# Nine one-hot tables and single-sample grams in a DLRM interaction tower

## The reference

```python
e = stack([tbl_t[ids[:, t]] for t in range(26)], axis=1)         # 2048 x 26 x 128
combined = concatenate([dense[:, None, :], e], axis=1)           # 2048 x 27 x 128
inter = einsum('bfd,bgd->bfg', combined, combined)[:, iu, ju]    # 351 pairs, iu < ju
h = concatenate([dense, inter, dense], axis=1)                   # 607 columns
h = maximum(h @ W_top1 + b_top1, 0)                              # 512
h = maximum(h @ W_top2 + b_top2, 0)                              # 256
y = h @ W_top3                                                   # 1
```

## Time and profile before

| | us |
|---|---|
| median of three runs | 413.59 (409.7 to 418.95) |
| profiled execution | 417.99 |
| its span in the trace | 416.2 |
| PE busy | 375.6 |
| DVE busy | 259.6 |
| POOL busy | 277.9 |
| ACT busy | 117.8 |

### The profile page before, as it was taken

The page is one execution under the profiler, slowest core; times in us unless marked ns, Lnnn a source line. Parts: engine busy times, 40 slices in busy tenths (PEclk is TensorE's granted clock), DMA queues, the critical chain, the costliest instruction groups (busy, mean ns, idle before and its releaser), DMA issues.

```text
span 416.2 us, 7055 instructions
## 1 busy us (share of the span) xinstructions
PE 375.6 (90%) x2906; PEld 339.9 (82%) x2906; DVE 259.6 (62%) x377; ACT 117.8 (28%) x255; POOL 277.9 (67%) x295
## 2 busy tenths in 40 slices
PE   0779998697989999999999999999999998889897
PEld 0768998697979898789879896989889886776787
DVE  4799989477766767577757585767657240521420
ACT  2442234222242232222332221322332132231120
POOL 6787778777777777777777777777777777720000
PEclk9999999999999999999999999999999998999856
DMA  7999444444333345334343444335333342310000
GB/s 178 262 280 257 106 98 91 77 78 92 78 78 60 73 91 101 83 81 90 78 82 77 89 83 102 79 56 116 56 53 52 56 78 51 58 25 2 1 2 0
DMA packets 51294, 35.91 MB, mean 86 GB/s; under 512 B 6488, under 2 KB 45016, under 8 KB 51264
## 3 DMA queue, kind: packets, MB, share of 16 engines
q0 software_dynamic: 41472, 18.89, 25.8%
q1 hardware_dynamic: 9792, 16.58, 15.4%
HBM read 35.44 MB, written 0.01 MB: 85 GB/s over the span
## 4 chain that ended last, share of the span: by engine, by line
POOL 42%; PE 38%; issue 15%; DMA 3%; ACT 1%; DVE 1%; POOLq 0%
POOL E L264 42%; PE psG L382 10%; PE psB L355 7%; PE psB L435 5%; PE psB L442 5%; PE psB L395 4%; DMA E<-tbl,gidx 2%; PE psB L340 2%; PE psB L428 2%; PE psB L449 1%; PE psB L411 1%; DVE Zp_lo L649 0%; ACT ET L541 0%; DMA gidx<-gather_idx 0%; ACT Zp_hi L571 0%
## 5 line engine op out<-in xcount | busy, mean ns | idle before, releaser
L264 POOL DMA_INDIRECT E<-tbl,gidx x288 | 277.2, 962 | 89.2 <-issue 86.5
L616 DVE TENSOR_TENSOR one_hot<-oidx,psR 125x1024 fp32r<-125x1024 int32 x128 | 152.5, 1216 | 44.0 <-PE psB L355 39.8
L355 PE MATMUL psB<-one_hot,tab_hi 125*128 125x256 f32 x512 | 137.3, 302 | 16.4 <-DVE tab_lo L621 11.1
L355 PE MATMUL psB<-one_hot,tab_lo 125*128 125x256 f32 x512 | 129.7, 287 | 0.0
L355 PEld LDWEIGHTS psB<-one_hot,tab_hi 125*128 125x128 f32 x512 | 99.7, 195 | 18.5 <-issue 12.0
L382 PE MATMUL psG<-ET 128*108 128x108 f32 x1024 | 111.5, 264 | 1.0 <-issue 0.8
L382 PEld LDWEIGHTS psG<-ET 128*108 128x108 f32 x1024 | 106.5, 180 | 2.2 <-ACT Y L506 0.9
L638 DVE COPY_PREDICATED S<-own,psG 108x216 f32<-108x216 int32 x192 | 77.0, 401 | 42.5 <-ACT S L565 36.6
L355 PEld LDWEIGHTS psB<-one_hot,tab_lo 125*128 125x128 f32 x512 | 100.0, 195 | 0.2
L541 ACT COPY ET<-psB 128x512 f32<-128x512 f32 (+1 forms) x80 | 42.6, 544 | 61.1 <-PE psB L340 61.0
L565 ACT COPY S<-psG 108x216 f32<-108x216 f32 x64 | 21.7, 340 | 100.2 <-PE psG L382 99.8
(11 more groups left out here) (35 smaller groups left out, 165.6 us busy)
## 6 DMA issues: line engine op xcount, KB each, us to landing
oidx<-hot_idx SPq DMA_DIRECT2D x32, 256.0 KB, 3.5
E<-tbl,gidx POOLq DMA_INDIRECT x288
ET<-tbl SPq DMA_DIRECT2D x8, 448.0 KB
dense<-dense_pairs SPq DMA_DIRECT2D x8, 128.0 KB, 4.0
Zd<-dense_rows SPq DMA_DIRECT2D x4, 256.0 KB, 2.8
UH<-W_pairs SPq DMA_DIRECT2D x1, 768.0 KB, 11.8
S<-W_dense SPq DMA_DIRECT2D x1, 512.0 KB, 8.5
w<-W SPq DMA_DIRECT2D x1, 512.0 KB, 10.3
```

The source lines that it names most:

```text
L264: nc.gpsimd.indirect_dma_start(E[:, n % SLOTS, i, :], None, gathered[feature_and_tile(n, i)[0]].bitcast(f32r), bass.IndirectOffsetOnAxis(a ...
L355: product = nc.tensor.matmul(bank[:, t % 2 * DUO:(t % 2 + 1) * DUO], tab[0:ROWS_P, t, r, :], one_hot[0:ROWS_P, m % RING, kc, :], start=(r ...
L616: nc.vector.tensor_tensor(one_hot[0:ROWS_P, m % RING], ids, rows, ALU.is_equal).then_inc(hot_full[m % RING], 1)
```

## The change

- **Tables.** One table with 1250 rows (125 partitions x 10 rows) becomes a one-hot table too: nine of them, 17 gathered. 272 gathers instead of 288. A duo has 74 row groups instead of 64, in 19 chunks of three or four, so 1184 products of 256 columns instead of 1024. The ring of one-hot tiles has four places and DVE builds four ahead.
- **Grams.** Each sample has its own matmul: 26 columns loaded, 26 columns passed, read from `ET` with a step of four elements (16 bytes) since the four samples lie interleaved. The four of a j write to partitions 0, 32, 64 and 96 up. A fill is 16 j. ACT alone copies a fill, all samples in one instruction; the predicated copies are gone. The columns without a sample between 26 and 32 are cleared once by DVE.
- **Buffers.** `ET` is a ring of three tiles (32 j) instead of two duos; psB has five banks instead of three, psG two instead of four.
- **Rows.** The gathered rows and the identity that turns them are plain fp32, no longer fp32r.
- **Order.** Stage h takes the turns of tile h by a running number. The chunks of a later duo d run in stages 2d-1 and 2d: stage 0 has the 19 chunks of duo 0, stages 1 to 14 have 9 or 10 each. In stage 16 the last three parts of the large piece are mixed with the last grams and with the layers of the small piece.
- **Loads.** All nine raw tables are loaded at once into places of their own (the third tile of `ET`, `UH`, `S`, `w2`); SP waits for all of them to be split before it loads the weights.

```diff
-ROWS = 1000
-HOT_TABLES = 8
+HOT_TABLES = ((1000, 8), (1250, 1))
+ROWS_P = 125
...
-    M = GROUP * F
+    M = F - 1
+    LANE = P // GROUP
+    MT = P - LANE + M
...
-    G_SIZE = 8
+    G_SIZE = 16
...
-    RING = 3
+    ET_RING = 3
+    RING = 4
...
-    BANKS = 3
+    BANKS = 5
...
-            return grams + layers_of(h)
-        split = T_GROUPS // 2 + 1
-        turns = [("T", d * T_GROUPS + i) for i in (range(split, T_GROUPS) if late else range(split))]
-
-        hots = [("hot", d + 1, late * CHUNKS // 2 + c) for c in range(CHUNKS // 2)] if d + 1 < DUOS else []
+            first, second = layers(SUPERS - 1, 0)[-3:], layers_of(h)
+            return (grams[:1] + first[:1] + grams[1:] + first[1:2] + second[:2] + first[2:] + second[2:])
+        turns = turns_of(h)
+
+        hots = [("hot", d + late, c) for c in range(CHUNKS)] if d + late < DUOS else []
         if h == 0:
-            hots = [("hot", 0, c) for c in range(CHUNKS)] + hots
             return hots[:5] + spread(turns, hots[5:])
+        hots = hots[:CHUNKS // 2] if late else hots[CHUNKS // 2:]
...
-        E = sb("E", [P, SLOTS, 4, D], f32r)
-        ET = sb("ET", [P, 2, DUO // GROUP, F, GROUP], f32)
+        E = sb("E", [P, SLOTS, 4, D], f32)
+        ET = sb("ET", [P, ET_RING, TILE_J, F, GROUP], f32)
...
             def load_weights():
+                sp.wait_ge(lo_ready, NS)
...
-                    turned = nc.tensor.transpose(bank[:, i * P:(i + 1) * P].bitcast(f32r),
-                                                 E[:, n % SLOTS, i, :], ident_r[:, :])
+                    turned = nc.tensor.transpose(bank[:, i * P:(i + 1) * P],
+                                                 E[:, n % SLOTS, i, :], ident[:, :])
...
                 for a in range(G_SIZE):
-                    j = i * G_SIZE + a
-                    four = ET[:, d % 2, j].rearrange("p f s -> p (f s)")
-                    gram = nc.tensor.matmul(psG[g % 2][0:M, a // 4, a % 4 * M:(a % 4 + 1) * M],
-                                            four, four, start=True, stop=True)
+                    j = i % TILE_FILLS * G_SIZE + a
+                    for q in range(GROUP):
+                        gram = nc.tensor.matmul(psG[g % 2][q * LANE:q * LANE + M, a * M:(a + 1) * M],
+                                                ET[:, tile % ET_RING, j, 0:M, q],
+                                                ET[:, tile % ET_RING, j, 1:F, q], start=True, stop=True)
...
-                    turned = nc.tensor.transpose(bank[0:n, i * M:(i + 1) * M], S[0:M, js, c],
-                                                 ident[0:M, 0:M])
+                    turned = nc.tensor.transpose(bank[0:n, i * P:i * P + MT], S[0:MT, js, c - 1],
+                                                 ident[0:MT, 0:MT])
...
-            def empty_gram_first(d, i):
+            def empty_gram(d, i):
                 g = gram_number(d, i)
                 act.wait_ge(G_full[g % 2], g // 2 + 1)
-                nc.scalar.copy(gram_rows(d, i), gram_samples(g, 0)).then_inc(G_first[g % 2], 1)
+                nc.scalar.copy(gram_rows(d, i),
+                               psG[g % 2][0:MT, 0:G_SIZE * M].rearrange("p (a f) -> p a f", a=G_SIZE)
+                               ).then_inc(G_out[g % 2], 1)
...
-            def empty_gram(d, i):
-                g = gram_number(d, i)
-                dve.wait_ge(G_first[g % 2], g // 2 + 1)
-                for q in range(1, GROUP):
-                    mine = own[0:M, q:q + 1].bitcast(i32).unsqueeze(2).unsqueeze(3).to_broadcast([M, 2, 4, F])
-                    copied = nc.vector.copy_predicated(gram_rows(d, i), mine, gram_samples(g, q))
```

More of the change, by code:

```diff
@@ L28, in dlrm_program @@
     PARTS = M1 + M2 + 1
-    T_GROUPS = NG // 2
+    TILES = 2 * DUOS
+    T_GROUPS = TILES * NG // 4
     SLOTS = 5
-    G_SIZE = 8
+    G_SIZE = 16
     G_FILLS = DUO // GROUP // G_SIZE
[L34 to L38, removed]
-    RING = 3
-    ID_RING = 3
     TILE_J = P // GROUP
     TILE_FILLS = TILE_J // G_SIZE
+    ET_RING = 3
+    RING = 4
+    ID_RING = 3
     SPREAD_P = ROWS_P // 16 * 16
-    RAW = 6
-    BANKS = 3
+    BANKS = 5
+    TABLE_K = [table.shape[0] // ROWS_P for table in small]
+    TABLE_BASE = [sum(TABLE_K[:t]) for t in range(NS)]
+    K_KINDS = sorted(set(TABLE_K))
+    ROW_BASE = {k: sum(x for x in K_KINDS if x < k) for k in K_KINDS}
+    CHUNK_K = 4
+    CHUNK_LIST = []
+    for t, k in enumerate(TABLE_K):
+        pieces = -(-k // CHUNK_K)
+        ends = [k * (i + 1) // pieces for i in range(pieces)]
+        CHUNK_LIST += [(t, start, end - start) for start, end in zip([0] + ends, ends)]
+    CHUNKS = len(CHUNK_LIST)
+    HOT_FILLS = -(-NS // 2)
+    FILL_FIRST = [min(c for c in range(CHUNKS) if CHUNK_LIST[c][0] // 2 == i) for i in range(HOT_FILLS)]
+    FILL_LAST = [max(c for c in range(CHUNKS) if CHUNK_LIST[c][0] // 2 == i) for i in range(HOT_FILLS)]
+    FIRST = -(-2 * NG // 4) * 4
     COLUMNS = [range(1 + 4 * b, min(5 + 4 * b, F)) for b in range(-(-(F - 1) // 4))]
@@ L93, in layers_of, with turns_of @@
             own = layers(u, 0)[first[quarter]:first[quarter + 1]]
-            return own + (layers(SUPERS - 1, 0) if quarter == 3 else [])
+            return own + (layers(SUPERS - 1, 0)[:-3] if quarter == 3 else [])
         return layers(u, 0)[LAYERS_FROM[quarter]:LAYERS_FROM[quarter + 1]]
+    def turns_of(h):
+        return [("T", n) for n in range(T_GROUPS) if 4 * n // NG == h]
     def steps_of(h):
@@ L125, in place_fills @@
         for i, step in enumerate(STEPS):
-            if step[0] == "gram" or (step[0] == "hot" and step[2] % FILL_CHUNKS):
+            if step[0] == "gram" or (step[0] == "hot" and step[2] not in FILL_FIRST):
                 continue
@@ L257, in _ @@
             pool.wait_ge(gidx_in[0], 16)
-            for n in range(DUOS * T_GROUPS):
-                if n == T_GROUPS:
+            for n in range(T_GROUPS):
+                if n == FIRST // 4:
                     pool.wait_ge(gidx_in[1], 16)
@@ L278, in load_table @@
             def load_table(h):
-                rows = small[h].rearrange("(p k) d -> p (k d)", k=ROWS_K)
+                rows = small[h].rearrange("(p k) d -> p (k d)", k=TABLE_K[h])
                 for part in (slice(0, SPREAD_P), slice(SPREAD_P, ROWS_P)):
                     sp.dma_start(raw_table(h)[part], rows[part]).then_inc(table_in[h], 16)
-            first = T_GROUPS * 4
-            sp.dma_start(gidx[:, 0:first], gather_idx[:, 0:first]).then_inc(gidx_in[0], 16)
+            sp.dma_start(gidx[:, 0:FIRST], gather_idx[:, 0:FIRST]).then_inc(gidx_in[0], 16)
             load_oidx(0)
-            for h in range(RAW):
+            for h in range(NS):
                 load_table(h)
@@ L308, in _ @@
                 for step in steps_of(h):
-                    if step[0] == "hot" and step[2] % FILL_CHUNKS == FILL_CHUNKS - 1:
-                        n = chunk_number(step[1], step[2]) // FILL_CHUNKS + ID_RING
-                        if n < DUOS * CHUNKS // FILL_CHUNKS:
+                    if step[0] == "hot" and step[2] in FILL_LAST:
+                        n = step[1] * HOT_FILLS + FILL_LAST.index(step[2]) + ID_RING
+                        if n < DUOS * HOT_FILLS:
                             m = chunk_number(step[1], step[2])
@@ L548, in place_dense @@
                 act.wait_ge(dense_in[d % 2], 16 * (d // 2 + 1))
-                nc.scalar.copy(ET[:, d % 2, :, 0, :], dense[:, d % 2].rearrange("p (j s) -> p j s", s=GROUP)
-                               ).then_inc(dense_out, 1)
+                for half in range(2):
+                    placed = nc.scalar.copy(ET[:, (2 * d + half) % ET_RING, :, 0],
+                                            dense[:, d % 2, half * P:(half + 1) * P].rearrange(
+                                                "p (j s) -> p j s", s=GROUP))
+                placed.then_inc(dense_out, 1)
             def empty_hot(d, c):
@@ L674, in _ @@
                             build_one_hot(m)
-                    elif step[0] == "gram":
-                        empty_gram(step[1], step[2])
                     elif step[0] == "C" and not on_scalar(step[3]):
@@ L695 @@
     batch = x["ids"].shape[0]
-    small = [t for t in range(_TABLES) if x[f"tbl_{t}"].shape[0] == ROWS][:HOT_TABLES]
+    small = [t for rows, many in HOT_TABLES
+             for t in [t for t in range(_TABLES) if x[f"tbl_{t}"].shape[0] == rows][:many]]
     gathered = [t for t in range(_TABLES) if t not in small]
```

188 lines of the change are left out of this document (88 added, 100 removed).

## The result

The changed kernel takes 409.95 us against 414.25 (medians of 20 runs each): a ratio of 0.9884, with a 95% interval of 0.9843 to 0.9926. Measured again later, it came out at 0.9925 [0.9879, 0.9971]. So it gains about 1%, within the 2% that count as no change, where 391 us and a gain of 5% were forecast. The profiled execution has a span of 406.9. Executions of one kernel differ by some 2% with the clock that PE was granted, and the ratios compare the faster ones of both kernels.

What follows compares the result with a forecast made beforehand. PE and POOL were taken as two bounds of nearly equal height. PE: 325.4 plus 57 + 6 for new grams gave 388; POOL: 387; 5 added for mutual disturbance gave span 393, time 391 us, range 382 to 440.

Steps and rivals of the forecast that it cites:

- the price of a gram record: PE, new grams: two loads beside each other, 14 ns a record, 57 us for 4096; bounds 8.5 and 25 ns.
- the change of shape at each fill: PE, 64 changes over between thin grams and full-width products: 0.1 us each, 6 us, from 0 to 17.
- rival 2: PE's grams: the 16-byte step slows the passing side, 44 ns a record, span 512, or 22 ns shared; chance 0.07.
- Rival 1: PE's grams: records stay serial, 25 ns each, 103 us for 97 before, time 431 us, slower; chance 0.29.
- The gathers' pace: POOL paces itself at 1.266 us a gather, still with 0.3 us of issue between; last ending at 348.
- the price of a one-hot product inside a chunk: PE's one-hot products: still 0.120 us each, 204 more after the start, +24.5 us.
- Plain turns: PE's turns of gathered rows in plain fp32: no extra cost, up to 272 x 0.02 = 5 us.
- Sum: 416.2 - 97.3 + 24.5 - 4 - 12 - 2: PE's span: old grams, start, gather waits and tail off, one-hot products added, 325.4 us before the new grams.
- the sum's 388: PE's span: 325.4 plus 57 for the new grams and 6 for changes of shape, 388 us.
- the start (-4): Start, on DVE: fewer builds before duo 0's last product, first gram at 42 instead of 46.35 us, -4.
- 32 fills of a different shape ... 6 us: PE, thin-gram fills among full-width products: 64 changes over at 0.1 us, 6 us, from 0 to 17.
- POOL's own bound ... Together 387: POOL: 272 gathers ending at 347.7 us, plus the work behind the last gather, a bound of 387 us.

Runs made afterwards that it cites:

- a_head: The changed kernel with one one-hot chunk put ahead of the first gram fill of each stage: ratio 0.9989 to the kernel before, span 411.5 us.
- a_half: The changed kernel with the grams of samples 2 and 3 of each four left out: ratio 0.9482 to the kernel before, span 394.9 us.
- a_contig: The changed kernel with each gram's 26 columns read from neighbouring elements (wrong columns), on a slower chip: 8.5 ns a record at the higher clock.
- a_fp32r: The changed kernel with gathered rows and their identity back in fp32r, on a slower chip: ratio 1.046 to the kernel before there.
- b_plain: The kernel before with gathered rows and identity in plain fp32: ratio 1.0049 to the kernel before.

## Why the prediction was wrong

**Right, in part by luck.** The step on which everything seemed to hang, the price of a gram record, was forecast at 14 ns and is 13.7; the change of shape at each fill was forecast at 6 us and is 7 (0.09 us ahead of a fill and 0.13 behind it). The reason for the 14 was wrong: I thought of two loads side by side at 25 ns serial. It is four groups with the step of 16 bytes in them; without the step it would be 8.5 at the higher clock. So rival 2 was there in part, with 4.8 ns for the step: too much overlap left out and no price for the step met in one number. Rival 1, serial, did not come; it would have been 50 ns, worse than I priced it. The gathers' pace (0.3 us of issue between them) and the price of a one-hot product inside a chunk (eight in 0.96 us) are as forecast. DVE ended at 211.1 for 208. Plain turns cost 5 us by the rows, the upper end that I gave.

The failure is in the sum. Here is PE's time, counted from the start of each record to the next, with idle time of over 0.15 us taken apart, and the forecast's terms shared out in the same way (us):

| | forecast | measured |
|---|---|---|
| to the first gram of the fifth tile | -17 | -2.5 |
| from there to the end | -11 | -6.7 |
| of which: records of the grams | -25.5 | -26.5 |
| one-hot products | +19.7 | +23.1 |
| idle time in and ahead of gram bursts | 0 | +9.2 |
| layers, records and idle time | -2 | -13.6 |
| waits for gathers and the rest | -3 | +1.2 |

**Wrong, the step "Sum: 416.2 - 97.3 + 24.5 - 4 - 12 - 2".** It takes every saving of PE for time, from the start on. But through the first 125 us PE can't be ahead of POOL (its last wait for a gather stands at 122.6 us in the changed kernel), and no kernel here, whatever was done to it, has its fifth tile's grams more than 4 us before the kernel before. The sum counted 17 us there: a quarter of the grams' gain, the start and most of the waits for gathers, less 5 for more one-hot products. It is the largest error, 15 of the 19 us between the sum's 388 and the span.

**Wrong in sign, the start (-4).** It was +4.5: the index loads stand behind the tables on SP's queue, which I had costed only for the weights. Undoing it moved the first gram by 5.6 us and the end by 1.1. So my -4 would not have reached the end either.

**Wrong, the term "32 fills of a different shape ... 6 us".** The changes of shape are in it, but it has no part for stops in the middle of a burst. They are 10.8 us by the rows, 6.4 of them behind the first gram of the fifth tile, where they count. That they come from long bursts is shown from three sides: fewer with shorter bursts, more with longer ones, none with half the records in each. That it is the supply of instructions rests on the traces: every stop ends 1.2 to 1.7 us after a packet of instructions. No row shows PE's own buffer, and no run changed the supply alone.

**A wait that I passed over.** At eight stages PE stands 0.57 to 0.83 us for ACT's last copy into ET, 5.9 us in all, because the chunks of a duo now end right ahead of its grams. a_head took them away, but lost more by it; alone it is not measured.

**What offset the second half.** The layers took 13.6 us less, of which I had 2. Their products are nearly the same. In the kernel before they ran at a mean granted clock of 0.68 at the end, in the changed kernel at 1.00, and part of their idle time was covered by mixing the steps; the two are not told apart. The clock's part is luck of the two profiled executions: their spans differ by 9.3 us, the medians only by 4.3.

**Wrong, the step "POOL's own bound ... Together 387".** I put the tail behind the last gather together from parts, 39 us, and none of the traces has it so short: 416.2 - 367.9 = 48.3 before, 48.5 after, 43.0 in a_half. But each holds work in which PE was behind POOL (last gather issued at 357.5, last turn at 379.15 in the changed kernel; 351.0 and 362.62 in a_half), so none of them is a bound by POOL. That bound is not measured, and it isn't what the changed kernel stands at: its chain is PE for 79% and POOL for 2%.

## What to carry to other kernels

When two engines bound a kernel, ask in which stretch each does: what the one saves where the other sets the pace is lost, and a sum over the whole span hides it. Compare a price only between rows at the same granted clock; at the lower one the step of 16 bytes looked like 1.5 ns, at the higher it was 4.8. A matmul made four times smaller becomes four times as many instructions; long runs of very short ones stop in mid-stream, and the cure is to cut them into shorter bursts with long instructions between, which here gave 10 us for one constant, 4 to 7 of them stops. A gain at the start counts only if the engine that it frees is the one that sets the pace there.

## What the runs showed of the hardware

- Records of 26 loaded and 26 passed fp32 columns, read with a step of 16 bytes, cost 50 ns in one group of 32 output partitions, 25 in two in turn, 13.3 to 13.7 in four; one group has 50 at either level of PE's clock.
- Read contiguously, four groups in turn cost 8.5 ns a record at the higher clock and 12.2 at the lower (a_contig), against 13.3 and 13.7 with the step (a_fp32r).
- A packet of 16 KB on the instruction queue goes with some 255 loads and matmuls of PE (48 packets for 12244, 23 for 5812). Bursts of 128 short matmuls stopped at such boundaries for up to 3.0 us, bursts of 256 for up to 3.4, and PE went on 1.2 to 1.7 us after the packet's end; with 64 at 25 ns there was no stop.
- An indirect gather of 128 rows of 512 bytes makes 144 packets into an fp32r tile and 32 into an fp32 one (41472 for 288 on the page of before, 9216 for 288 in b_plain; after, 8704 for 272, 17.6% of the DMA engines' time instead of 25.8%). The pace of POOL did not change with it.
